# Four graph layers on one core: edges 2 gathers projected node rows of 768 bytes, and edges 0 takes 18 VectorE steps

## The chip, the cores and the metric

The kernel runs on one core of one Trainium2 chip. The metric is the time of one execution on the device in microseconds (us). The core has five engines that run side by side and meet at semaphores: TensorE (PE in the profile, its weight loads PEld), VectorE (DVE), ScalarE (ACT), GpSimd (POOL) and SyncE (SP), which here only issues DMAs. Sixteen DMA engines move the data. SBUF and PSUM are the two on-chip memories; TensorE writes only to PSUM.

## The reference

A graph of 12,500 nodes and 200,000 edges, sorted by their destination `dst`, goes through four layers, each followed by a sum with `x` and a layer norm. Every layer makes something per edge from a row of its source node and from edge attributes, sums it over each destination's edges (in three layers with a softmax over these edges), and does some work per node. The change is about the third layer, L2, and a little about the first, L0:

```python
# L0 (16 values per head, 4 heads)
scores = jnp.einsum('ehd,ehd->eh', q[edge_src], k[edge_dst]) / np.sqrt(D)
agg = segment_sum(softmax_over_dst(scores)[:, :, None] * v[edge_src], edge_dst)

# L2: h = x, eh = edge_attr_64, qrh = edge_attr_64_n2, qeh = edge_attr_64_n3, one head, d = 64
se = jnp.concatenate([h[src], eh], axis=-1)
msg = jax.nn.leaky_relu(se @ W_msg, 0.01)
q = jnp.concatenate([qrh, qeh], axis=-1) @ W_q / temp      # temp = 8
k = se @ W_k
att = jnp.sum(q * k, axis=-1)
alpha = softmax of att over the edges of each dst
agg = jax.ops.segment_sum(alpha[..., None] * msg, dst, num_segments=N)
hn = leaky_relu(agg @ W_out) + h    # then a layer norm; nodes without edges keep h
```

Everything is float32.

## The kernel before

**Stages.** The program is a row of blocks, one after the other: setup and search (indices, the q, k, v projections of L0), then for each layer an edge phase and a node phase: edges 0, nodes 0, edges 1, nodes 1, edges 2, nodes 2, edges 3, nodes 3. A block begins when all engines have ended the one before. Each partition holds 1,568 edges in a row and 98 nodes in a row (`edges_pp`, `nodes_pp`).

**An edge phase** (`class EdgePhase`) works in 56 chunks of `J` = 28 columns; a column is 128 edges, one per partition. For each column GpSimd issues one indirect DMA (L774) that gathers 128 rows of a table by source node: 1,568 gathers in a phase. The chunks alternate between two buffers `b`; a buffer is given back by the semaphore `rows_free[b]`. SP loads attributes and stores the running sums. VectorE and ScalarE make scores, a running maximum along the edges, exponentials, and a scan that sums over the edges of a destination; `lay_out` on ScalarE turns the sums around for the store to `sums`. After the last chunk, `Chained` repairs destinations whose edges lie in two partitions (L971 to L974), and only then does the node phase gather the last sum of every node: 98 gathers (L1671).

**Edges 2 before** (`edge_phase_2`, L1274): the gathers bring rows of `x` (64 floats, 256 bytes) from `p.x_tables[1]` into the left half of `se`; ScalarE copies the edge attribute into the right half (L1403). For each four columns (`QUAD`) TensorE turns `se` and the two query attributes (L1338, L1342), ScalarE moves them out of PSUM (L1386, L1387), TensorE multiplies with `w2_mk` (message and key side by side, L1356) and with `w2_qr`, `w2_qe` (L1358, L1359), ScalarE takes the results (L1394, L1396), and VectorE multiplies query and key (L1457), makes the leaky message from the PSUM tile and the copy `msg` (L1458) and reduces the score (L1461). Once per chunk follow the running softmax (L830 to L836), the weighting of `msg` (L1471) and five scans (L892). The last chunk is cut at column `ph.cut` = 20, so that its first part is summed and stored while the rest is made (`part_of_last`, L1478).

**Nodes 1 before** (`node_phase_1`, L2004) has two passes over 15 groups of nodes (13 of `G` = 7 columns, then 4 and 3). The first goes with the 98 gathers and collects the batch-norm sums. Then comes the point at which all engines need the moments (L2147 to L2174). The second pass: ScalarE applies scale and ReLU (`light`, L2102), TensorE turns back and centres (`turn_back`, L2075), VectorE adds to `x` (L2180), ScalarE squares (L1710), VectorE sums (L1715), ScalarE takes the root (L1720), VectorE inverts it (`turn_over`, L1733), GpSimd scales the rows (L2050), and SP stores them as the table for edges 2 (L1680). The order in which each engine takes these stages is set by `in_turn(groups, (lag, stage), ..., per=)`: stage `lag` steps behind, one group every `per` steps.

**Edges 0 before** (`edge_phase_0`, L1042): per chunk one scan per head for the running maximum (L830), one multiplication per head for the values (L1115), one scan per head for the sums (L892).

## Time and profile before

| what | value |
|---|---|
| median of 3 runs | 9007.13 us (9006.42 to 9010.77) |
| time of the profiled execution | 9015.53 us |
| its span, first to last instruction | 9013.6 us |
| edges 0, gathers by edge (335 to 2240) | 1905 us |
| edges 1 (2537 to 4499) | 1962 us |
| nodes 1 with the tail of edges 1 (4499 to 4714) | 215 us |
| edges 2 (4714 to 6677) | 1963 us |
| nodes 2 with the tail of edges 2 (6677 to 6888) | 211 us |
| edges 3 (6888 to 8845) | 1957 us |

Times within the trace are us from the start of the span. A row of an instruction gives its start, its duration, the engine, the line, what it writes from what, the shape, and in brackets how long its engine stood idle before it and for whom. Of GpSimd's instructions the gathers are the busy ones; "issue" is time in which it waited for nothing that the profile shows. A row such as `x8` holds eight instructions that follow each other. A float32 product on TensorE stands in the trace as two MATMUL instructions.

### The profile page before, as it was taken

How to read it: one execution, taken by the hardware profiler on the slowest of the kernel's cores; microseconds unless marked ns; L12 is line 12 of the kernel's file. 1: busy time of each engine (PE TensorE's matmuls, PEld its weight loads, DVE VectorE, ACT ScalarE, POOL GpSimd, SP SyncE). 2: the span in 40 equal slices, each digit the busy share in tenths (PEclk: the TensorE clock that was granted, in tenths of full speed). 3: DMA queues.
4: the chain of work that ended last, by engine and by line, in shares of the span. 5: the costliest groups of instructions: out<-in, count | busy, mean ns of one | idle time of the engine just before them, and what ended most of it. 6: DMA issues, size and time to landing. Idle time of an engine off the chain costs nothing. (4 is left out here: it accounts for less than half of the span.)

```text
span 9013.6 us, 55519 instructions
## 1 busy us (share of the span) xinstructions
PE 2221.6 (25%) x11915; PEld 1741.6 (19%) x11915; DVE 4945.2 (55%) x6681; ACT 3183.7 (35%) x3856; POOL 6621.2 (73%) x6997
## 2 busy tenths in 40 slices
PE   3000000000200000000046666666654222222224
PEld 1000000000200000000026666666643010101013
DVE  5356565656747777777744454544455333333335
ACT  0123222222513232232324555555544333333332
POOL 6777777777677777777757777777765777777776
PEclk6555555555555555555558888888877565656556
DMA  9233333333123333333323443434322333333332
GB/s 359 81 111 105 111 107 109 109 109 112 35 77 105 111 102 114 102 114 102 105 79 121 131 136 129 138 128 139 125 86 76 124 114 124 114 122 116 121 117 82
DMA packets 367105, 1037.47 MB, mean 115 GB/s; under 512 B 164320, under 2 KB 172410, under 8 KB 352272
## 3 DMA queue, kind: packets, MB, share of 16 engines
q1 hardware_dynamic: 136048, 670.35, 19.9%
q0 software_dynamic: 224608, 342.26, 15.6%
q10 hardware_dynamic: 6336, 23.79, 0.7%
q14 instruction: 96, 0.79, 0.0%
q8 instruction: 17, 0.28, 0.0%
HBM read 634.02 MB, written 401.90 MB: 115 GB/s over the span
## 5 line engine op out<-in xcount | busy, mean ns | idle before, releaser
L774 POOL DMA_INDIRECT g<-x_table,edge_ix x1512 | 1426.9, 944 | 460.8 <-issue 460.8
L774 POOL DMA_INDIRECT se<-x_table,edge_ix x1512 | 1426.8, 944 | 460.8 <-issue 460.8
L774 POOL DMA_INDIRECT hidden<-hidden_table,edge_ix x1512 | 1426.6, 943 | 460.8 <-issue 460.8
L774 POOL DMA_INDIRECT qv<-qv_table,edge_ix x1484 | 1400.3, 944 | 452.3 <-issue 452.3
L902 ACT ACTIVATE edge_sums<-edge_val 128x1904 f32<-128x1904 f32 (+3 forms) x220 | 1115.2, 5069 | 459.8 <-DVEq L1597 459.8
L892 DVE TENSOR_TENSOR_SCAN edge_val<-edge_bank,edge_val 128x464 f32<-128x464 f32 (+1 forms) x715 | 687.7, 1033 | 360.1 <-ACT edge_val L1559 353.6
L1551 PE MATMUL edge_e_ps<-w_nodes,edge_ea_t 128*128 128x512 f32 x784 | 477.9, 776 | 1464.6 <-DVEq L1591 1456.1
L845 ACT ACTIVATE edge_bank<-edge_weight_arg 128x112 f32<-128x112 f32 (+3 forms) x169 | 38.6, 228 | 2114.5 <-DVE edge_decay_arg L836 2114.5
L892 DVE TENSOR_TENSOR_SCAN edge_val<-edge_decay,edge_val 128x493 f32<-128x493 f32 (+1 forms) x672 | 714.2, 1132 | 13.4
L1590 DVE TENSOR_TENSOR hidden<-hidden,edge_e_ps 128x3584 f32<-128x3584 f32 x55 | 213.9, 3888 | 843.5 <-DMA hidden<-hidden_table,edge_ix 792.9
L1457 DVE TENSOR_TENSOR edge_product<-mk_ps,edge_q_now 128x256 f32<-128x256 f32 x392 | 166.5, 425 | 900.3 <-ACT edge_msg L1396 899.1
L1559 ACT ACTIVATE edge_val<-hidden 128x3584 f32<-128x3584 f32 x55 | 348.4, 6335 | 786.7 <-DVEq L1591 786.7
L1104 DVE TENSOR_TENSOR edge_product<-edge_k_ps,qv 128x896 f32<-128x896 f32 x112 | 185.7, 1658 | 642.4 <-DMA qv<-qv_table,edge_ix 635.4
L1551 PEld LDWEIGHTS edge_e_ps<-w_nodes,edge_ea_t 128*128 128x128 f32 x784 | 192.4, 254 | 1750.0 <-DVEq L1591 1501.6
L1029 PE MATMUL edge_k_ps<-ident,edge_fix_wide 128*128 128x128 f32 x8 | 2.1, 441 | 2092.7 <-DVEq L989 2092.7
L1356 PE MATMUL mk_ps<-w_mk,edge_se_t 128*128 128x128 f32 x3136 | 480.9, 302 | 141.9 <-ACT edge_q_t L1387 122.1
L1029 PE MATMUL edge_bond_ps<-ident,edge_fix_wide 128*128 128x128 f32 x4 | 1.2, 462 | 2041.7 <-DVEq L989 2041.7
L1671 POOL DMA_INDIRECT node_rows<-sums,end_index x392 | 374.9, 956 | 129.5 <-issue 118.2
L1356 PEld LDWEIGHTS mk_ps<-w_mk,edge_se_t 128*128 128x128 f32 x3136 | 429.8, 212 | 179.5 <-ACT edge_q_t L1387 140.8
L1338 PE MATMUL se_ps<-ident,se 128*128 128x128 f32 x1568 | 304.0, 327 | 535.9 <-ACT se L1403 354.1
L1029 PEld LDWEIGHTS edge_k_ps<-ident,edge_fix_wide 128*128 128x128 f32 x8 | 1.8, 328 | 2092.8 <-DVEq L989 2092.8
L1029 PEld LDWEIGHTS edge_bond_ps<-ident,edge_fix_wide 128*128 128x128 f32 x4 | 0.9, 323 | 2041.8 <-DVEq L989 2041.8
(418 smaller groups left out, 8264.4 us busy)
## 6 DMA issues: line engine op xcount, KB each, us to landing
sums<-edge_sums SPq DMA_DIRECT2D x56, 1848.0 KB, 7.1
sums<-edge_sums SPq DMA_DIRECT2D x55, 1792.0 KB, 6.3
sums<-edge_sums SPq DMA_DIRECT2D x56, 1008.0 KB, 4.3
sums<-edge_sums SPq DMA_DIRECT2D x55, 924.0 KB, 3.8
edge_k<-k_edges SPq DMA_DIRECT2D x56, 896.0 KB, 4.6
edge_bond<-in_edge_attr SPq DMA_DIRECT2D x56, 896.0 KB, 8.3
edge_eh<-in_edge_attr SPq DMA_DIRECT2D x56, 896.0 KB
edge_qr<-in_edge_attr_n SPq DMA_DIRECT2D x56, 896.0 KB
```

The source lines that it names most:

```text
L774: e.indirect_dma_start(self.gather_into(u, j), None, self.gather_from, bass.IndirectOffsetOnAxis(ap=now[:, j:j + 1], axis=0))\
L845: e.activation(self.weight[:, :, now], self.weight_arg[:, :, now], ACT.Exp).then_inc(self.weighed, 1)
L892: return e.tensor_tensor_scan(out=now, data0=keep[:, 0:n, :].rearrange("p f j -> p (f j)"), data1=now, initial=0.0, op0=ALU.mult, op1=ALU.add)
L902: e.activation(self.sums[b][:, :, 0:n], self.val[b][:, :, 1:].rearrange("p f j -> p j f"), ACT.Copy)\
L1104: e.tensor_tensor(product[:, 32 * half:32 * half + 32, :], k_ps[:, :, 1:], q[:, 32 * half:32 * half + 32, :], ALU.mult)
L1338: e.transpose(se_ps[u][:, j, :], se[b][:, QUAD * c + j, :], p.ident[:, :])
L1356: e.matmul(mk_ps[u][:, j, :], se_t[u][:, j, :], p.w2_mk[:, :], start=True, stop=True)
L1457: e.tensor_tensor(product[:, now, :], mk_ps[u][:, :, FD:], q_now[u][:, :, :], ALU.mult)
L1551: last = e.matmul(e_banks[:, q, :], ea_t[b][:, q, :], p.w3_e, start=True, stop=True)
L1559: e.activation(ph.val[b][:, :, 1:], g[b].rearrange("p j f -> p f j"), ACT.Relu).then_inc(taken, 1)
L1590: e.tensor_tensor(g[b][:, :, :], g[b][:, :, :], e_ps, ALU.add)
L1671: e.indirect_dma_start(self.rows[:, t, :], None, self.p.sums[self.layer], bass.IndirectOffsetOnAxis(ap=self.p.end_index[:, t:t + 1], axis=0))\
```

## The change

**Edges 2.** The score is rewritten: q · k = (attributes of the query) · (`W_q` `W_k`^T applied to `se`). Nodes 1 makes, for every node, a row of 192 floats, `x W_msg` (64) and `x W_k W_q^T / 8` (128, "points"), and stores it in `pair_table` (768 bytes a row). Edges 2 gathers these rows. TensorE makes only the part of the edge attribute, from attributes that are turned on the host (`eh_t`, one product of 384 columns for two columns of edges, `p.w2_e`), in six `pieces` of 4, 4, 6, 4, 4 and 6 columns over a ring of seven PSUM banks. VectorE adds the gathered points into the PSUM tile, adds the gathered message part into `msg` (SBUF), multiplies the points with the 128 query attributes (`q_in`, loaded as they are) and reduces. The leaky step is one instruction per chunk on `msg`, behind the running softmax. The transposes, ScalarE's copies and the query product are gone. `rows_free` and `attr_free` are now given by VectorE after the last piece. `cut` is 18.

**Nodes 1.** The weights are prepared at its start (loads, two transposes, two products, copies). The second pass gets, behind GpSimd's scaling, `turn_x` and `project` on TensorE and `move_x` and `take_x` on ScalarE; the store comes from `pair_out`. `in_turn` goes by `per=4`.

**Edges 0** (`merged=True`): one scan for the running maximum of all heads, one multiplication for all values, one scan for all sums; the penalty row is a copy per head in SBUF; the factor 0.25 moves from every chunk into the query weights in the setup, for which TensorE now waits (`s_quartered`). `part_summed` comes from the one scan.

```diff
@@ edge_phase_2 @@
-                e.tensor_tensor(product[:, now, :], mk_ps[u][:, :, FD:], q_now[u][:, :, :], ALU.mult)
-                e.scalar_tensor_tensor(msg[:, now, :], mk_ps[u][:, :, 0:FD], 0.01, msg[:, now, :],
-                                       ALU.mult, ALU.max).then_inc(scored, 1)
-                e.drain()
-                e.tensor_reduce(score[:, 0, now], product[:, now, :], AX.X, ALU.add)
+                e.wait_ge(made, at(i, 2 * per, per * b + k + 1))
+                e.tensor_tensor(points, two(g[b][:, cols, FD:]), points, ALU.add)
+                e.tensor_tensor(two(msg[:, cols, :]), two(g[b][:, cols, 0:FD]), values, ALU.add)
+                e.drain()
+                e.tensor_tensor(two(product[:, 0:slot, :]), two(q_in[b][:, cols, :]), points, ALU.mult)
+                e.drain().then_inc(used, 1)
+                e.tensor_reduce(ph.score[:, 0, cols], product[:, 0:slot, :], AX.X, ALU.add)
+                e.drain()
 
             def chunk(i, b):
...
+                for k in range(per):
+                    weigh(i, b, k)
+                e.sem_inc(ph.rows_free[b], 1)
+                e.sem_inc(ph.attr_free[b], 1)
                 ph.carry_values(e, i, b)
                 ph.running_softmax(e, i, b)
+                e.scalar_tensor_tensor(msg[:, :, :], msg[:, :, :], 0.01, msg[:, :, :], ALU.mult, ALU.max)
+                e.drain()
                 ph.wait_decay(e, i, b)
@@ node_phase_1, TensorE @@
+            def project(g):
+                e.wait_ge(x_moved, g + 1)
+                after(e, x_taken, g)
+                for k in range(firsts[g]):
+                    last = e.matmul(pair_banks[:, k, :], x_t[g % 2][:, k, :], p.w2_x, start=True, stop=True)
+                last.then_inc(x_done, 1)
-            in_turn(groups, (1, turn_back))
+            in_turn(groups, (1, turn_back), (8, turn_x), (10, project), per=4)
@@ node_phase_1, ScalarE @@
+            def move_x(g):
+                n = firsts[g]
+                e.wait_ge(x_turned, g + 1)
+                after(e, x_done, g - 1)
+                e.activation(x_t[g % 2][:, 0:n, :], x_ps[:, 0:n, :], ACT.Copy).then_inc(x_moved, 1)
             in_turn(groups,
                     (0, light),
                     (3, lambda g: norm.act_square(e, g, p.x[:, ph.now(g), :])),
-                    (5, lambda g: norm.act_root(e, g, p.eps[:, 0:1])))
+                    (5, lambda g: norm.act_root(e, g, p.eps[:, 0:1])),
+                    (9, move_x),
+                    (11, take_x), per=4)
@@ edge_phase_0 @@
-                    for n in range(4):
-                        last = ph.scan_rows(e, b, rows * n, rows, decay[:, n, :, :])
-                        if n == 1:
-                            last.then_inc(ph.part_summed, 1)
+                    sums = ph.val[b].rearrange("p f j -> p (f j)")
+                    e.tensor_tensor_scan(out=sums, data0=decay_flat, data1=sums, initial=0.0,
+                                         op0=ALU.mult, op1=ALU.add).then_inc(ph.part_summed, 1)
```

How the instructions stand now. ScalarE in the second pass of nodes 1, before (`node_held` is `light`, `node_rows` the square, `node_var` the root):

```order
L2102 ACTIVATE node_held<-node_held,node_bn 128x512 x3
L1710 ACTIVATE node_rows<-x_now 128x7x64
L2102 ACTIVATE node_held<-node_held,node_bn 128x512
L1710 ACTIVATE node_rows<-x_now 128x7x64
L2102 ACTIVATE node_held<-node_held,node_bn 128x512
L1720 ACTIVATE node_var<-node_var,eps 128x7
L1710 ACTIVATE node_rows<-x_now 128x7x64
```

The same place after; `node_x_t` is `move_x`, `node_pair_out` is `take_x`:

```order
L2088 ACTIVATE node_held<-node_held,node_bn 128x512
L2094 ACTIVATE node_x_t<-node_work 128x512
L1658 ACTIVATE node_var<-node_var,eps 128x7
L2102 ACTIVATE node_pair_out<-node_work 128x1152
L2105 ACTIVATE node_pair_out<-node_work 128x192
L1648 ACTIVATE node_rows<-x_now 128x7x64
L2088 ACTIVATE node_held<-node_held,node_bn 128x512
```

Three `light` instructions ran ahead before; now each stands behind the `take_x` of a group that is three behind it, with the square between them.

TensorE in the same pass, before and after; before there are only the 56 products of `turn_back`:

```order
L2081 MATMUL node_fold_ps<-node_moments,node_fold 128x2
L2082 MATMUL node_fold_ps<-node_moments,node_fold 128x1
L2075 MATMUL node_back_ps<-node_centred,node_held 128x128 x56
```

```order
L2043 MATMUL node_work<-ident,x_now 128x128 x3
L2046 MATMUL node_work<-ident,x_now 64x128
L2035 MATMUL node_back_ps<-node_centred,node_held 128x128 x4
L2053 MATMUL node_work<-w_nodes,node_x_t 128x384 x4
L2043 MATMUL node_work<-ident,x_now 128x128 x3
L2046 MATMUL node_work<-ident,x_now 64x128
L2035 MATMUL node_back_ps<-node_centred,node_held 128x128 x4
L2053 MATMUL node_work<-w_nodes,node_x_t 128x384 x4
```

`turn_x` of a group, `turn_back` of the group two ahead and `project` of the group now follow each other.

VectorE in edges 2, before, the steps of one `QUAD` (`edge_product` is query times key, `edge_score` the reduced score):

```order
L1457 TENSOR_TENSOR edge_product<-mk_ps,edge_q_now 128x256
L1458 SCALAR_TENSOR_TENSOR edge_msg<-mk_ps,edge_msg 128x256
L1461 TENSOR_REDUCE edge_score<-edge_product 128x4
```

After, from the last piece of a chunk to the weighting of the messages:

```order
L1389 TENSOR_TENSOR edge_pair_ps<-pair,edge_pair_ps 128x3x2x128
L1390 TENSOR_TENSOR edge_msg<-pair,edge_pair_ps 128x384
L1392 TENSOR_TENSOR edge_product<-edge_q_in,edge_pair_ps 128x768
L1394 TENSOR_REDUCE edge_bank<-edge_product 128x6
...
L855 TENSOR_TENSOR edge_decay_arg<-edge_bank,edge_peak 128x28
L1404 SCALAR_TENSOR_TENSOR edge_msg<-edge_msg 128x1792
...
L1407 TENSOR_TENSOR edge_val<-edge_msg,edge_bank 128x64x28
```

The leaky step was made seven times a chunk from a PSUM tile; it now stands once, behind the running softmax, and reads `msg` alone.

## Rows read from the trace of the kernel before

**Rows 1.** The page's first part: busy time, share, instructions of each engine.
```profile
PE 2221.6 (25%) x11915; PEld 1741.6 (19%) x11915; DVE 4945.2 (55%) x6681; ACT 3183.7 (35%) x3856; POOL 6621.2 (73%) x6997
```
**Rows 2.** Busy time by stage: stretch, length, engines (instructions), clock, DMA share, GB/s.
```profile
4499.00:4714.00 215.00, 89.31 (x284) 52.17 (x284) 88.26 (x185) 53.20 (x101) 107.93 (x116) 0.60 0.22 64
4714.00:6677.00 1963.00, 1298.52 (x9368) 1224.81 (x9368) 961.34 (x1947) 999.30 (x1893) 1485.02 (x1568) 0.86 0.41 132
6888.00:8845.00 1957.00, 477.92 (x784) 192.43 (x784) 724.40 (x612) 714.95 (x111) 1479.41 (x1568) 0.60 0.37 118
```
**Rows 3.** Groups of gathers; the last is that of nodes 1, rows of 528 bytes.
```profile
L774 POOL DMA_INDIRECT se<-x_table,edge_ix x1512 | 1426.8, 944 | 460.8 <-issue 460.8
L774 POOL DMA_INDIRECT hidden<-hidden_table,edge_ix x1512 | 1426.6, 943 | 460.8 <-issue 460.8
...
L1671 POOL DMA_INDIRECT node_rows<-sums,end_index x98 | 92.6, 945 | 31.9 <-issue 29.6 <-POOLq L1169 2.4
```
**Rows 4.** Timeline of nodes 1, a group in the second pass, then its end.
```profile
4695.08 0.80 ACT L2102 ACTIVATE node_held<-node_held,node_bn 128x512 f32<-128x512 f32 x1
4696.20 0.58 ACT L1710 ACTIVATE node_rows<-x_now 128x448 f32<-128x448 f32 x1
4696.27 1.13 PE L2075 MATMUL node_back_ps<-node_centred,node_held 128*128 128x128 f32 x8 [0.47 <-DVE x_now L2180]
4696.68 0.80 ACT L2102 ACTIVATE node_held<-node_held,node_bn 128x512 f32<-128x512 f32 x1
...
4705.74 2.87 POOL L2050 TENSOR_TENSOR x_now<-x_now,node_var 128x448 f32<-128x448 f32 x4 [0.40 <-DVEq L1734]
...
4713.81 0.99 POOL L774 DMA_INDIRECT se<-x_table,first_src  x1 [5.21 <-POOLq L2498]
```
**Rows 5.** The second pass as two stretches: all of it, and its steady middle.
```profile
4680.60:4713.80 33.20, 16.90 (x112) 14.81 (x112) 19.62 (x48) 21.73 (x45) 13.17 (x15) 0.81 0.26 97
4689.00:4699.00 10.00, 7.23 (x53) 6.06 (x51) 8.48 (x20) 9.33 (x20) 5.99 (x7) 1.00 0.37 137
```
**Rows 6.** Prices: products of 512 columns in setup at either clock, ScalarE copies.
```profile
21.57 5.44 PE L597 MATMUL proj_ps<-w_nodes,x_t 128*128 128x512 f32 x8
...
27.28 3.60 PE L597 MATMUL proj_ps<-w_nodes,x_t 128*128 128x512 f32 x8
...
L1386 ACT ACTIVATE edge_se_t<-se_ps 128x512 f32<-128x512 f32 x392 | 234.1, 597 | 319.2 <-PE q_ps L1342 302.5 <-issue 8.8 <-DVEq L1449 7.9
...
L2068 PE MATMUL node_h_ps<-node_tile_t,node_w_pair 128*128 128x384 f32 x26 | 19.1, 837 | 0.0
```
**Rows 7.** Timeline: VectorE with both inputs in SBUF, and gathers.
```profile
4720.74 2.03 DVE L1445 TENSOR_TENSOR edge_product<-bc_L_gnn_beta,live 128x1792 f32<-128x1792 f32 x1
4721.35 2.25 POOL L774 DMA_INDIRECT se<-x_table,first_src  x1 [0.30 <-issue]
4722.85 2.03 DVE L1448 TENSOR_TENSOR aux_now<-aux_now,edge_product 128x1792 f32<-128x1792 f32 x1
4723.91 1.78 POOL L774 DMA_INDIRECT se<-x_table,first_src  x1 [0.30 <-issue]
...
6743.91 0.62 DVE L2306 SCALAR_TENSOR_TENSOR node_other<-node_other 128x448 f32<-128x448 f32 x1
6744.09 1.26 POOL L1671 DMA_INDIRECT node_rows<-sums,end_index  x1 [0.30 <-issue]
```
**Rows 8.** VectorE groups in edges 2, and in edges 0 (last).
```profile
L892 DVE TENSOR_TENSOR_SCAN edge_val<-edge_bank,edge_val 128x377 f32<-128x377 f32 x275 | 235.3, 922 | 6.4
L1471 DVE TENSOR_TENSOR edge_val<-edge_msg,edge_bank 128x1792 f32<-128x1792 f32 x55 | 179.0, 3255 | 42.4 <-ACT edge_bank L848 42.4
L1461 DVE TENSOR_REDUCE edge_score<-edge_product 128x4 f32<-128x256 f32 x392 | 164.7, 420 | 36.3
...
L1115 DVE TENSOR_TENSOR edge_val<-qv,edge_bank 128x448 f32<-128x448 f32 x220 | 185.7, 906 | 18.3 <-ACT edge_bank L845 18.3
```
**Rows 9.** Timeline of the end of edges 2.
```profile
6675.65 0.95 POOL L774 DMA_INDIRECT se<-x_table,edge_ix  x1 [0.30 <-issue]
...
6694.48 0.33 SPq L742 DMA_DIRECT2D sums<-edge_sums  x1
...
6705.37 0.97 POOL L1671 DMA_INDIRECT node_rows<-sums,end_index  x1 [2.29 <-POOLq L1280]
```

More of the change, by code:

```diff
@@ L1374, in _ @@
+                    for k, cols in enumerate(pieces):
+                        e.wait_ge(used, at(i, 2 * per, per * b + k + 1))
+                        for n, bank in enumerate(range(slots[k % ring].start, slots[k % ring].stop)):
+                            last = e.matmul(banks[:, bank, 0:2 * wide], eh_t[b][:, cols.start // 2 + n, :],
+                                            p.w2_e[:, :], start=True, stop=True)
+                        last.then_inc(made, 1)
             chained.tensor(e)
@@ L1480, in part_of_last @@
                 i, now = ph.rounds - 1, ph.columns(more)
-                for c in range(now.start // QUAD, now.stop // QUAD):
-                    weigh(i, 1, c)
-                e.drain()
-                e.tensor_scalar(ph.score[:, :, now], score[:, :, now], 0.125, None, ALU.mult)
+                for k in range(per):
+                    if now.start <= pieces[k].start < now.stop:
+                        weigh(i, 1, k)
                 e.memset(cut_decay(more)[:, :, :, 0], 0.0)
@@ L2038, in _ @@
         def _(e):
-            for g in range(groups):
-                ph.store(e, g, p.x_tables[1])
-            e.wait_ge(ph.out, 16 * groups)
+            e.dma_start(w_k[:, :], p.ins["L2_gnn_W_k"]).then_inc(w_in, 16)
+            e.dma_start(w_q[:, :], p.ins["L2_gnn_W_q"]).then_inc(w_in, 16)
+            e.wait_ge(w_zeroed, 1)
+            for n in range(2):
+                for k, to in enumerate((p.w2_x, p.w2_e)):
+                    e.dma_start(to[n * FD:(n + 1) * FD, n * wide:n * wide + FD],
+                                p.ins["L2_gnn_W_msg"][k * FD:(k + 1) * FD, :]).then_inc(w_in, 16)
+            table = p.pair_table.rearrange("(p t) f -> p t f", p=P)
+            for g in range(groups):
+                e.wait_ge(x_taken, g + 1)
+                e.dma_start(table[:, ph.now(g), :], pair_out[g % outs][:, 0:ph.sizes[g], :])\
+                    .then_inc(stored[g % outs], 16)
+            for u in range(outs):
+                e.wait_ge(stored[u], 16 * len(range(u, groups, outs)))
         @block.gpsimd
```

321 lines of the change are left out of this document (158 added, 163 removed).

## Prediction

> **What bounds the kernel.** I began with the page's busy line [rows 1]: GpSimd is busy 73% of the span, no other engine more than 55%. That is an average, so next came busy time by stage [rows 2]. In edges 2, 1,963 us long, GpSimd is busy for 1,485 us with 1,568 gathers, TensorE for 1,299, ScalarE for 999, VectorE for 961. The groups of instructions [rows 3] give the rest of GpSimd's time: a gather is busy for 944 ns, and in front of each lie 460.8/1,512 = 0.305 us of "issue", in which it waits for nobody. 0.944 + 0.305 = 1.249 us, times 1,568 is 1,958 us: the whole stage. So edges 2 is a bare stream of gathers, and edges 3 is the same stream (943 ns, 1,957 us) with TensorE at 478 us instead of 1,299. What the change takes from TensorE and ScalarE in edges 2 lies behind this stream and is worth nothing there. Three things count: what lies between streams, what delays GpSimd inside one, and what would outgrow the 35.0 us that 28 gathers take.
>
> Between the streams I read the timeline of nodes 1 [rows 4]. From the point at which all engines have the moments (4680.60) to the first gather of edges 2 (4713.81) lie 33.2 us [rows 5] in which GpSimd has only 15 short scalings. No gather can start before the last row of the table is stored, so each microsecond added here is a microsecond of the kernel.
>
> **Edges 2, the stream.** Rows grow from 256 to 768 bytes. The trace has 256 bytes (944 ns), 512 (943) and 528 (945) [rows 3]: no slope, so 0 is taken. The mean DMA share is 0.41 with rows of 256 bytes and 0.37 with 512 and fewer attributes [rows 2]; tripled rows bring it to about 0.55 by my estimate, with room left. A loss, if transfers did back up, is a rival below.
>
> VectorE per chunk: with both inputs in SBUF 448 elements take 0.62 us and 1,792 take 2.03 [rows 7], so 1.05 ns an element and 0.15 fixed. A piece of 4 columns is three instructions over 512 elements and one over 256: 3 x 0.69 + 0.42 = 2.5, 2.65 with its drains; a piece of 6 by the same 3.6. Four and two of them are 17.8 us. Then the small instructions of the softmax with their waits for ScalarE, about 1.9 (an estimate), the leaky step 2.0, the weighting 3.26 and five scans 235.3/55 = 4.3 [rows 8]: 29.3 us of 35.0. Hidden, with 5.7 us to spare; TensorE's 14 products of 384 columns, 28 instructions at 0.73 us even at half clock [rows 6], are 20 us, hidden too.
>
> **The leaky step delays a gather.** In before it read PSUM and `msg`; now it reads `msg` twice, 1,792 columns, 2.03 us. At the start of edges 2 the timeline [rows 7] shows what such an instruction does: VectorE runs from 4720.74 to 4722.77 with both inputs in SBUF, and the gather begun at 4721.35 takes 2.25 us, not 0.94; it ends 0.83 us behind VectorE. The second pair (4722.85 + 2.03; 4723.91 + 1.78) ends 0.81 behind, and in nodes 2 an instruction of 0.62 us from 6743.91 makes the gather of 6744.09 take 1.26, again 0.82 behind. So a gather needs something 0.13 us after its start, and if VectorE is in such an instruction then, it waits for its end. Within the chunks of before only instructions with an input in PSUM run, and the gathers keep their 944 ns [rows 3]. The new step comes once in each of 55 whole chunks. If its phase against the gathers is random, a gather starts 0 to 1.249 us into it; the stretch is what is left of 2.03, on average 2.03 - 0.62 = 1.4 us: **+77 us**. The phase is in fact nearly fixed within a chunk, since VectorE starts its last piece on the last gather's landing; my sum for the step's start, about 7.6 us behind that, falls right beside a gather's need, and I can't tell which side. The ends are 0.78 us a chunk (+43) and 2.0 (+111).
>
> **Nodes 1, second pass.** Before, a group costs 1.6 us (`light` 4695.08 to 4696.68 [rows 4]), TensorE being in its 8 instructions for 1.13 of it. The middle shows 7.23 us of TensorE in 10 at clock 1.00 [rows 5]. After, ScalarE's order puts `light` of a group behind `take_x` of one three behind, `take_x` waits for `project`, and TensorE's order puts `project` behind the `turn_back` that needs that `light`. That closes a ring with no overlap:
> take_x, 1,152 and 192 columns, by 0.597 for 512 [rows 6]: 1.5; square 0.5; light 0.75; turn_back 1.13; project, 8 instructions of 384 columns, by 3.60/8 x 384/512 = 0.34 each: 2.7. That is 6.6, with five hand-overs of 0.1 **7.1 us a group**. At half clock turn_back is about 2.0 and project 8 x 0.66 = 5.3 (between 0.51 = 5.44/8 x 0.75 and 0.73 [rows 6]): 10.6 us.
> TensorE is in the ring's work (turn_back, project, and turn_x beside take_x) for some 5 of 7.1 us, the share that stands beside full clock in [rows 5], so I take the warm price. The pass: two groups of filling 8.1, one cycle in which group 0 goes down its whole chain (norm, scaling 2.87, transpose, move) 9.2, twelve cycles 85.2, less 1.3 for the two short groups, the last project and take 5.2, and from there to the first gather 5.2 as before's last wait [rows 4]. Together 111.6 us instead of 33.2: **+78.5**. Below: if the ring overlapped fully, TensorE's 5.1 us a group would bound it, some 88 us, +55. Above: at half clock twelve cycles cost 3.5 more each, +120.
>
> **Small terms.** The weights' preparation at the start of nodes 1 lies beside 98 gathers (98 x 1.25 = 122 us [rows 3]): 0. In setup TensorE waits for two more VectorE scalings, some 2.5 us; VectorE's and GpSimd's later idle time takes it up: 0, at most 1. Edges 0: `lag` now reads SBUF twice for about 0.3 us a chunk; by the rule above it would rarely meet the need of a gather, 0 taken, at most 15. Its nine fewer instructions a chunk are hidden but in the last; between 0 and 9 x 0.15 I take -0.6. The tail of edges 2: before, the store goes out at 6694.48, 17.9 us after the last gather's end [rows 9]. After, on the same clock: the cut part is done by 6678.8 (my sum, from the landing of its last column), two pieces 6.25, softmax 1.5, leaky 0.8, weighting 1.2, scans 1.8, turning around 1.2: 6691.6, **-2.9**.
>
> **Sum.** Profiled execution 9015.5 + 78.5 + 77 - 2.9 - 0.6 = 9167.5, +152. That execution is 8.4 us above the median of 9007.1, so the median becomes 9159 us.
>
> **Rivals.**
> 1. The clock stays at its half level in the second pass: the ring has waits that before's middle has not. The whole pass stands at 0.81 [rows 5], nodes 1 as a whole at 0.60 [rows 2]. +120 instead of +78.5: about 9200.
> 2. VectorE becomes the bound in edges 2, or rows of 768 bytes back up. For it: 5.7 us of margin rest on estimates, and PSUM accesses may cost more than SBUF's. Each microsecond a chunk over 35.0 costs 56 us, so one that is over by 1 gives 9215, and up from there. Against: the sum of 29.3 would have to be off by a fifth.
> 3. No stretch, because the leaky step falls where no gather needs anything or the rule is something else: 9159 - 77 = 9082.
> 4. Not slower. ScalarE's 999 us and TensorE's 1,299 in edges 2 slow each gather, and without them its 1.249 us shrinks. To cancel 152 us it must lose 152/1,568 = 97 ns; with 1.15 us the time is about 9004. Against: edges 3 has 715 and 478 us of the same work and the same 943 ns [rows 2, 3].
> 5. The change doesn't do what it says, for instance the ring isn't closed because the order of the two engines leaves slack: +55 instead of +78.5, 9136; this is inside the forecast's own range.
>
> **How the numbers follow.** Forecast (with 5) 0.72, clock 0.09, VectorE or transfers 0.08, no stretch 0.07, not slower 0.04. The forecast's own bounds are the stretch at 43 or 111 and the pass at +55 or +78.5: 9102 to 9193. The range takes in the missing stretch below and the low clock with a long stretch above, 9080 to 9225. A run of this kernel can tell 0.2%, 18 us, from no change. Only rival 4 comes there: faster 0.03, same 0.02; slower 0.95.
>
> **What would show it.** The stretch: in edges 2 one gather a chunk of 1.7 to 2.9 us, ending about 0.8 behind the leaky step, all others at 944 ns; GpSimd busy about 1,560 us and the stage about 2,040. The pass: first gather of edges 2 about 110 us behind the moments, ScalarE's `light` every 7.1 us, its wait ended by TensorE's `project`. I am wrong if VectorE and not "issue" ends GpSimd's idle time in edges 2, if gathers without a VectorE instruction beside them differ from 944 ns, or if the pass shows half clock.

## The result and the profile after

| what | before | after |
|---|---|---|
| median of 4 runs, us | 9008.95 | 9134.59 |
| lowest and highest | 9006.42, 9013.25 | 9130.21, 9136.48 |
| ratio, 95% interval | | 1.0137 (1.0124 to 1.0150) |
| span of the profiled execution | 9013.6 | 9132.2 |

The changed kernel is 1.4% slower, 125.6 us in the medians against 152 forecast. The spans of the two profiled executions differ by 118.6 us. By the first and last gathers of the stages, that difference lies here:

| stretch | before, us | after, us | difference |
|---|---|---|---|
| start to the end of the last gather of nodes 1 | 4666.9 | 4668.9 | +2.0 |
| from there to the first gather of edges 2 (contains the second pass) | 46.9 | 118.6 | +71.8 |
| first to last gather of edges 2 | 1962.8 | 2017.3 | +54.5 |
| tail of edges 2, to the first gather of nodes 2 | 28.8 | 25.1 | -3.7 |
| nodes 2, to the first gather of edges 3 | 182.6 | 178.9 | -3.7 |
| edges 3 and nodes 3 | 2125.6 | 2123.3 | -2.3 |

The last two rows are code that the change doesn't touch. Their 6.0 us are about the 6.6 us by which before's profiled execution lies above the median of its runs. The row of nodes 2 wanders by that much in any case: in the four variants of the next section, where its code is the same, it is 178.1 to 181.8 us. The page's busy line, to be held against [rows 1]:

```profile
PE 1872.5 (21%) x4249; PEld 957.9 (10%) x4249; DVE 5454.6 (60%) x6299; ACT 2476.6 (27%) x2302; POOL 6676.1 (73%) x6997
```

Three stages in the windows view, against [rows 2] (stretch, length, busy time and instructions of TensorE, its weight loads, VectorE, ScalarE, GpSimd, then clock, DMA share, GB/s):

```profile
4501.00:4787.50 286.50, 141.59 (x458) 84.17 (x458) 92.03 (x193) 78.31 (x146) 107.78 (x116) 0.67 0.21 71
4787.50:6805.00 2017.50, 916.40 (x1568) 419.43 (x1568) 1510.68 (x2130) 269.31 (x305) 1539.94 (x1568) 0.67 0.53 179
7008.80:8966.00 1957.20, 476.39 (x784) 192.34 (x784) 725.41 (x612) 715.20 (x111) 1479.52 (x1568) 0.60 0.36 118
```

In edges 2 TensorE lost 382 us of work and ScalarE 730, VectorE gained 549, and the stage is as long as GpSimd's stream makes it: 2,017.5 instead of 1,963, with GpSimd 55 us busier. Its groups of gathers (against [rows 3]: 944 ns, 460.8 us of issue):

```profile
L783 POOL DMA_INDIRECT pair<-pair_table,edge_ix x1512 | 1480.5, 979 | 460.6 <-issue 460.6
L783 POOL DMA_INDIRECT g<-x_table,edge_ix x1512 | 1427.9, 944 | 460.8 <-issue 460.8
```

The issue time is what it was; the mean of a gather is 979 ns. In the view of the gathers' one line, the minimum, median and maximum of the same gathers show that this is no slope with the row size, but a few long ones:

```profile
L783 POOL DMA_INDIRECT pair<-pair_table,edge_ix x1512: 942/946/2046, 4864.1 to 6804.0; - x189
```

One chunk's timeline shows where the long one stands (start, duration):

```profile
5265.47 0.95 POOL L783 DMA_INDIRECT pair<-pair_table,edge_ix  x1 [0.30 <-issue]
5265.71 0.19 DVE L855 TENSOR_TENSOR edge_decay_arg<-edge_bank,edge_peak 128x28 f32<-128x28 f32 x1
5265.81 2.01 DVE L1404 SCALAR_TENSOR_TENSOR edge_msg<-edge_msg 128x1792 f32<-128x1792 f32 x1
...
5266.72 1.92 POOL L783 DMA_INDIRECT pair<-pair_table,edge_ix  x1 [0.30 <-issue]
```

The leaky step runs to 5267.82; the gather of 5266.72 needs something at 5266.85 and ends 0.98 us late, at 5268.64, which is 0.82 behind the step's end, as in [rows 7]. All 55 steps do this, with stretches of 0.84 to 1.10 us, 51.2 us in all. The other 3 us of the stage are the median of a gather, 946 instead of 944 ns, times 1,568.

The second pass of nodes 1, ScalarE's timeline of one group (against [rows 4]):

```profile
4743.35 1.13 ACT L2102 ACTIVATE node_pair_out<-node_work 128x1152 f32<-128x1152 f32 x1 [3.15 <-PE node_work L2053]
4744.38 0.33 ACT L2105 ACTIVATE node_pair_out<-node_work 128x192 f32<-128x192 f32 x1
4744.59 0.58 ACT L1648 ACTIVATE node_rows<-x_now 128x448 f32<-128x448 f32 x1
4745.05 0.81 ACT L2088 ACTIVATE node_held<-node_held,node_bn 128x512 f32<-128x512 f32 x1
...
4749.69 1.13 ACT L2102 ACTIVATE node_pair_out<-node_work 128x1152 f32<-128x1152 f32 x1 [3.15 <-PE node_work L2053]
```

And TensorE's, of the same group and of one 13 us later:

```profile
4745.92 1.16 PE L2035 MATMUL node_back_ps<-node_centred,node_held 128*128 128x128 f32 x8 [2.17 <-ACT node_held L2088]
4746.91 2.75 PE L2053 MATMUL node_work<-w_nodes,node_x_t 128*128 128x384 f32 x8
...
4758.61 1.87 PE L2035 MATMUL node_back_ps<-node_centred,node_held 128*128 128x128 f32 x8 [2.17 <-ACT node_held L2088]
4760.28 3.74 PE L2053 MATMUL node_work<-w_nodes,node_x_t 128*128 128x384 f32 x8
```

The ring is there: ScalarE waits 3.15 us for `project`, TensorE 2.17 us for `light`, and `take_x` comes every 6.34 us (4743.35, 4749.69). The last two rows are a group in which `turn_back` and `project` take 1.87 and 3.74 us instead of 1.16 and 2.75; every third or fourth group is such a one. The windows view gives the granted clock of the two groups, 1.00 and 0.72 (third number from the end):

```profile
4745.90:4752.20 6.30, 4.18 (x20) 2.80 (x20) 1.45 (x3) 3.15 (x7) 0.94 (x1) 1.00 0.26 108
4758.60:4764.80 6.20, 5.84 (x20) 3.95 (x20) 0.82 (x2) 1.38 (x3) 0.94 (x1) 0.72 0.21 84
```

### The profile page after: what moved, and what is told of

Its sections match the earlier page's. It is cut to its first block and busy times, and to the rows that moved or that the text cites. A ratio compares the mean times of both kernels' runs of the same rounds, so it can differ in the third digit from the quotient of the medians.

```text
span 9132.2 us, 36460 instructions
## 1 busy us (share of the span) xinstructions
PE 1872.5 (21%) x4249; PEld 957.9 (10%) x4249; DVE 5454.6 (60%) x6299; ACT 2476.6 (27%) x2302; POOL 6676.1 (73%) x6997
## 5 line engine op out<-in xcount | busy, mean ns | idle before, releaser
L783 POOL DMA_INDIRECT pair<-pair_table,edge_ix x1512 | 1480.5, 979 | 460.6 <-issue 460.6
L783 POOL DMA_INDIRECT g<-x_table,edge_ix x1512 | 1427.9, 944 | 460.8 <-issue 460.8
L783 POOL DMA_INDIRECT hidden<-hidden_table,edge_ix x1512 | 1426.7, 944 | 460.8 <-issue 460.8
L1340 PE MATMUL edge_pair_ps<-w_e,edge_eh_t 128*128 128x384 f32 x1568 | 916.4, 749 | 1101.4 <-DVEq L1393 1086.3
L1340 PEld LDWEIGHTS edge_pair_ps<-w_e,edge_eh_t 128*128 128x128 f32 x1568 | 419.4, 287 | 1597.8 <-DVEq L1393 1329.5
L1389 DVE TENSOR_TENSOR edge_pair_ps<-pair,edge_pair_ps 128x512 f32<-128x512 f32 x336 | 263.8, 785 | 401.1 <-DMA pair<-pair_table,edge_ix 315.0
L911 DVE TENSOR_TENSOR_SCAN edge_val<-edge_decay,edge_val 128x493 f32<-128x493 f32 x448 | 467.4, 1117 | 6.7
L920 ACT ACTIVATE edge_sums<-edge_peak 128x112 f32<-128x112 f32 (+2 forms) x165 | 50.2, 304 | 1269.9 <-DVEq L1257 669.8
L1228 DVE TENSOR_TENSOR g<-g,edge_bond_ps 128x1792 f32<-128x1792 f32 x56 | 113.2, 2021 | 430.4 <-DMA g<-x_table,edge_ix 394.7
L1246 DVE TENSOR_TENSOR edge_val<-g,edge_bank 128x1792 f32<-128x1792 f32 x112 | 351.6, 3179 | 16.1 <-ACT edge_bank L864 16.1
```

Source lines behind the costliest of these rows:

```text
L783: e.indirect_dma_start(self.gather_into(u, j), None, self.gather_from, bass.IndirectOffsetOnAxis(ap=now[:, j:j + 1], axis=0))\
L911: return e.tensor_tensor_scan(out=now, data0=keep[:, 0:n, :].rearrange("p f j -> p (f j)"), data1=now, initial=0.0, op0=ALU.mult, op1=ALU.add)
L1228: e.tensor_tensor(g[b][:, :, :], g[b][:, :, :], bond_ps[:, :, :], ALU.add)
L1246: e.tensor_tensor(ph.values(b)[:, n, :, :], rows_now, bcast(ph.weight[:, n, :], 1, FD), ALU.mult)
L1340: last = e.matmul(banks[:, bank, 0:2 * wide], eh_t[b][:, cols.start // 2 + n, :], p.w2_e[:, :], start=True, stop=True)
L1389: e.tensor_tensor(points, two(g[b][:, cols, FD:]), points, ALU.add)
```

## Experiments on the two terms

Four variants of the changed kernel ran on one chip, where the kernel before took 9,009.2 us; beside the changed kernel itself, 9,134.59 us, it had taken 9,008.95. Theory A: a gather needs something 0.13 us after its start, and then waits for the end of a VectorE instruction that is running with both inputs in SBUF. The rivals: the time that VectorE spends in such instructions counts, wherever it stands (B), or any long VectorE instruction does it (C).

**The leaky step in two parts.**

```diff
-                e.scalar_tensor_tensor(msg[:, :, :], msg[:, :, :], 0.01, msg[:, :, :], ALU.mult, ALU.max)
-                e.drain()
+                for m in (msg[:, 0:13, :], msg[:, 13:J, :]):
+                    e.scalar_tensor_tensor(m, m, 0.01, m, ALU.mult, ALU.max)
+                    e.drain()
```

> The changed kernel, with the leaky step of edges 2 in two instructions, of 13 and 15 of the 28 columns, at the same place. In the trace of the changed kernel each of the 55 steps stretches one gather by 0.84 to 1.11 us, 51 us in all; the step of 5265.81 + 2.01 meets the gather of 5266.72. Theory A (a gather needs something 0.13 us after its start, and waits for the end of the VectorE instruction with two SBUF inputs that is running just then): the first part would run from 5265.81 to 5266.83, the gather needs at 5266.85, the second part would run from about 5266.9 to 5268.05, the next gather needs at 5268.10. Both parts miss, the stretch falls from 0.93 to 0 to 0.15 us a chunk, and the time falls by 43 to 51 us, to about 9087. Theory B (what counts is how long VectorE reads two SBUF inputs beside a gather, wherever the gather stands): the same 2.1 us a chunk, the same 51 us, the time stays within 5 us of 9135.

Measured 9084.13 us, 50.5 less than the changed kernel. One chunk's timeline:

```profile
5327.53 0.95 POOL L783 DMA_INDIRECT pair<-pair_table,edge_ix  x1 [0.30 <-issue]
...
5327.91 2.25 DVE L1405 SCALAR_TENSOR_TENSOR edge_msg<-edge_msg 128x832 f32<-128x832 f32 x2
...
5328.78 0.95 POOL L783 DMA_INDIRECT pair<-pair_table,edge_ix  x1 [0.30 <-issue]
5330.04 0.94 POOL L783 DMA_INDIRECT pair<-pair_table,edge_ix  x1 [0.30 <-issue]
```

The page's group of the gathers:

```profile
L783 POOL DMA_INDIRECT pair<-pair_table,edge_ix x1512 | 1429.9, 946 | 460.5 <-issue 460.5
```

VectorE spends 2.25 us here, more than before the split, and no gather of the chunk is stretched by more than 0.01 us: the first part (1.01 us) ends at 5328.92, the gather needs at 5328.91, and the second part ends at 5330.16, where the next gather needs at 5330.17. The mean over all chunks is 946 ns, as the median. B falls.

**The leaky step 0.45 us sooner**, directly behind the scan of the running maximum instead of three short instructions later.

> The changed kernel, with the leaky step moved ahead by two short instructions, to directly behind the scan of the running maximum: it starts 0.45 us sooner, at 5265.36 instead of 5265.81 on the clock of that chunk, and ends 5267.37. Theory A: the gather that starts at 5265.47 needs something at 5265.60, now inside the step, and waits until 5267.37: a stretch of 1.77 us a chunk instead of 0.93, so 46 us more than the changed kernel, about 9180 (with a jitter of the phase of 0.15 us, 9170 to 9190). Theory B (duration alone counts) and the theory that gathers are slowed by rows of 768 bytes: no difference, 9135.

Measured 9180.71 us, 46.1 more than the changed kernel. The chunk:

```profile
5349.20 2.02 DVE L1405 SCALAR_TENSOR_TENSOR edge_msg<-edge_msg 128x1792 f32<-128x1792 f32 x1
5349.30 2.75 POOL L783 DMA_INDIRECT pair<-pair_table,edge_ix  x1 [0.30 <-issue]
```

The same instruction, moved by less than half a microsecond, now holds the gather from 5349.43 to 5351.22: 1.79 us, and over 55 chunks 95.9 us.

**One input in PSUM.** The step becomes a maximum of `msg` with a row of a PSUM bank, of the same length (2.01 us) at the same place. The variant leaves the leaky step out, so it doesn't compute the reference, and TensorE gets the bank of the last piece back only behind this instruction (`used`); the part of the edit that holds it back is left out here.

```diff
...
-                e.scalar_tensor_tensor(msg[:, :, :], msg[:, :, :], 0.01, msg[:, :, :], ALU.mult, ALU.max)
-                e.drain()
+                e.tensor_tensor(msg[:, :, :], msg[:, :, :], bcast(banks[:, slots[-1].start, 0:FD], 1, J), ALU.max)
+                e.drain().then_inc(used, 1)
```

> The changed kernel, with the leaky step of edges 2 replaced, at the same place, by a maximum of the same 1,792 elements with 64 values of a PSUM bank, repeated over the columns: same length, one input in SBUF, one in PSUM. It leaves the leaky step out. Theory A (two SBUF inputs are what a gather waits for): all gathers of the chunks back at 0.94 to 0.95 us, 51 us less, about 9084. Theory C (any long VectorE instruction at this place, or VectorE's load as a whole, holds the gather up): the same stretch, 9135.

Measured 9086.79 us, 47.8 less. The four runs lie between 9082.44 and 9103.45, and the profiled one is the longest; in it gathers have a median of 947 ns in stages that no edit touches too, 949 in edges 2. The chunk shows a gather that starts inside the instruction and keeps its length; so do those of all 55 chunks:

```profile
5336.91 2.01 DVE L1407 TENSOR_TENSOR edge_msg<-edge_msg,edge_pair_ps 128x1792 f32<-128x1792 f32 x1
...
5337.90 0.94 POOL L783 DMA_INDIRECT pair<-pair_table,edge_ix  x1 [0.30 <-issue]
```

C falls as well: at the same length and the same place, the second SBUF input makes the difference.

**Where theory A is wrong.** It says that a gather is held if its need, 0.13 us after its start, falls inside the instruction. In the trace of `leaky_split` there are 20 gathers whose need does fall inside the second part, but which start 0.02 to 0.13 us before it. One of them, and the second part beside it:

```profile
5363.78 0.95 POOL L783 DMA_INDIRECT pair<-pair_table,edge_ix  x1 [0.30 <-issue]
5363.87 1.16 DVE L1405 SCALAR_TENSOR_TENSOR edge_msg<-edge_msg 128x960 f32<-128x960 f32 x1
```

By theory A this gather waits from 5363.91 to 5365.03, and the 20 together are 22 us longer; none of them takes more than 0.95 us. Nine others start inside the first part with their need still ahead of its end, and are 0.29 us longer in all, where theory A gives 0.26. So the rule that the traces bear out has one more condition: a gather is held only if it starts while the instruction is running, and then until the instruction's end, from 0.13 us after the gather's start. The gain of the split rests on both, the needs at the ends of the parts and the gathers that were already under way when the second part began.

**The second pass in another order.** Only the lags change (turn_back 6, turn_x 16, project 21; light 1, square 10, root 12, move_x 16, take_x 23; add_x 7, sum 10, turn_over 12), so that `light` runs a group further ahead and `turn_x` and `move_x` of the next group stand before `project` and `take_x` of this one.

> The changed kernel, with another order in the second pass of nodes 1 and nothing else: light, turn_back and the norm run one group further ahead, turn_x of the next group stands before project of this one, and move_x before take_x. The trace of the changed kernel shows 6.35 us a group at full clock (every fourth or fifth about 8 us), in which ScalarE waits 3.15 us for project and TensorE 2.17 us for light. Theory A (the ring take_x, square, light, turn_back, project is what makes the pass long): without it TensorE is the bound, project 2.75, turn_back 1.16, turn_x 0.66 = 4.6 us a group, 5.1 with the slower groups: 11 groups x 1.85 = 20 us less, and up to 5 more at the ends; about 9110. Rival (the clock: with less waiting nothing else changes, but TensorE's work itself is the bound): nothing, 9135.

Measured 9106.94 us, 27.7 less; the first gather of edges 2 comes 88.2 us after the last of nodes 1 instead of 118.6. The windows row of the pass:

```profile
4682.60:4756.70 74.10, 59.02 (x274) 39.96 (x273) 20.72 (x48) 45.25 (x87) 13.29 (x15) 0.96 0.32 130
```

Two rounds of TensorE in its timeline:

```profile
4716.20 2.82 PE L2053 MATMUL node_work<-w_nodes,node_x_t 128*128 128x384 f32 x8 [0.21 <-ACT node_pair_out L2105]
4718.85 1.05 PE L2035 MATMUL node_back_ps<-node_centred,node_held 128*128 128x128 f32 x8
4719.75 0.49 PE L2043 MATMUL node_work<-ident,x_now 128*128 128x128 f32 x3
...
4720.55 2.82 PE L2053 MATMUL node_work<-w_nodes,node_x_t 128*128 128x384 f32 x8 [0.21 <-ACT node_pair_out L2105]
```

A group takes 4.35 us, TensorE waits 0.21 of them. The ring was worth 2.0 us a group; what is left is TensorE's own work. The slower groups are gone too, all twelve rounds between `take_x` of full groups are 4.35 us: the granted clock of the stretch is 0.96, where the pass of the changed kernel has this row:

```profile
4682.60:4787.60 105.00, 67.53 (x277) 45.32 (x276) 21.08 (x48) 45.90 (x89) 13.32 (x16) 0.89 0.23 92
```

## Runs on other chips

The other eight runs fell on four other chips, in four groups, and on each of them the kernel before takes 11,422 to 11,443 us. A time of these runs is compared only with that of before on the same chip. Gathers don't bound edges 2 of before on these chips, as shown below, so the times say little for or against the expectations that were made for a chip with 9,009 us.

> The kernel before, with one instruction added in each of the 55 whole chunks of edges 2, where the changed kernel has its leaky step: a maximum of msg with itself, 1,792 elements, two SBUF inputs, about 2.0 us. It changes no value. VectorE has some 17 us to spare in a chunk. Theory A (a gather waits from 0.13 us after its start to the end of such an instruction): from the trace of before it would start at 5325.30 in one chunk and end 5327.31, and the gather of 5326.06 needs at 5326.19: 1.12 us; in the chunk of 6023.45 the gather of 6023.97 would wait 1.36. So 62 to 75 us more than before, about 9078. Theory D (the step costs only in the changed kernel, whose rows of 768 bytes or whose VectorE load make gathers touchy): at most 5 us, 9009 to 9014.

> The kernel before, with the instructions of two SBUF inputs at the starts of edges 1 and edges 2 given one input in PSUM: the two scans of 1,568 elements that read same (copied to PSUM first), and beta times live and its addition to aux, in thirteen steps of eight nodes through PSUM. In before's trace these stretch gathers by 2.94 + 2.07 = 5.0 us in edges 1 and by six times 0.84 to 1.31 = 5.5 us in edges 2. Theory A: both go, 10 us less, about 8999. Rival (the copies and the additional steps hold up the first chunk instead): no change or up to 5 us more.

> The kernel before with the part of edges 0 and the setup alone: one scan for the running maximum, one multiplication, one scan for the sums, the factor 0.25 in the query weights. My prediction had 0 for the setup, 0 (at most +15) for the new addition of two SBUF inputs, and -0.6 for the tail. The trace of the changed kernel has the first gather of edges 0 0.6 us later, the stream itself 0.1 us shorter and the nodes' first gather 0.35 us later relative to it: +0.8 in all. Either way the time stays within 2 us of before; the trace tells which.

> The changed kernel with the leaky step in two parts, the other order in the second pass of nodes 1, and the starts of edges 1 and 2 without instructions of two SBUF inputs. If the three are independent: 9134.6 - 50.5 (as measured for the split) - 27.7 (as measured for the order) - 10 = 9046. If the stretches were one budget that something else then fills, or the phase of the chunks shifts so that the parts of the leaky step meet a gather again, up to 50 us more. In no case below before: the projection's TensorE time in nodes 1, some 40 us, stays.

> The kernel before with one maximum of msg with itself added in each of the 55 whole chunks of edges 2, at the place of the changed kernel's leaky step: 1,792 elements, two SBUF inputs, about 2.0 us; no value changes. It is run again because the chip of the first run has longer times throughout (11,425 us for the kernel before), with GpSimd waiting for TensorE in edges 2; this one is to tell on a chip with 9,009 for before. Theory A (a gather waits from 0.13 us after its start to the end of such an instruction): 1.12 and 1.36 us in the two chunks read in before's trace, so 62 to 75 us more than before, about 9078. Theory D (the step costs only in the changed kernel): at most 5 us, 9009 to 9014.

> The changed kernel with the leaky step in two parts, the other order in the second pass of nodes 1, and the starts of edges 1 and 2 without instructions of two SBUF inputs; again for the same reason. If the three are independent: 9134.6 - 50.5 - 27.7 - 10 = 9046. If the phase of the chunks shifts so that the parts of the leaky step meet a gather again, up to 50 us more. On a chip with 11,425 for before it should again be near 10,400.

> The changed kernel as it is, next to the kernel before. On the chip of the last two groups of runs before takes 11,425 to 11,443 us, and there edges 2 is not a stream: GpSimd pauses some 27 us in each chunk, for TensorE to give a buffer back. If what pauses it is the long way from a landed row through transposes, ScalarE and TensorE, the changed kernel, in which VectorE gives the buffer back behind six short pieces, gains there what the three variants together gained: 10,400 to 10,600 us, some 8% less than before. If that gain came from the three edits of the variant, the changed kernel is near before. On a chip with 9,009 for before it is 9,130 to 9,137 again.

> The kernel before with edges 0 and the setup as in the changed kernel, and with the starts of edges 1 and 2 free of instructions of two SBUF inputs: what the runs so far leave as candidates for a version below both kernels. On a chip with 9,009 us for before: the quiet starts take away 5.0 + 5.5 us of stretched gathers, the part of edges 0 adds 0.8: 9 to 10 us less, 8,999 to 9,001. On a chip with 11,425 for before: the part of edges 0 alone measured 20 us less there, the quiet starts alone nothing (0.9999): 11,405, ratio 0.998. If neither holds, no difference.

| kernel | us | before on the chip | ratio (95% interval) |
|---|---|---|---|
| changed kernel (changed_again) | 10419.8 | 11421.9 | 0.9126 (0.9111 to 0.9141) |
| changed, three edits (split_open_quiet) | 10402.3 | 11425.5 | 0.9102 (0.9090 to 0.9114) |
| the same (all_three_again) | 10429.1 | 11442.9 | 0.9113 (0.9098 to 0.9128) |
| before plus an instruction (before_two_sbuf) | 11275.1 | 11425.5 | 0.9866 (0.9851 to 0.9881) |
| the same (two_sbuf_again) | 11329.1 | 11442.9 | 0.9897 (0.9881 to 0.9914) |
| quiet starts (before_quiet) | 11424.9 | 11425.5 | 0.9999 (0.9990 to 1.0008) |
| edges 0 part alone (edges0_only) | 11405.3 | 11425.5 | 0.9983 (0.9974 to 0.9992) |
| edges 0 part and quiet starts (quiet_edges0) | 11415.8 | 11443.2 | 0.9977 (0.9968 to 0.9986) |

Of the expectations, that of `changed_again` came (10,400 to 10,600), and so did the ratio of 0.998 for `quiet_edges0`; `all_three_again` was to be near 10,400 and is 10,429. The added instruction was to cost 62 to 75 us and before got 150 and 114 us faster; the edges 0 part was to stay within 2 us and is 20 us faster; the quiet starts were to give 10 us and gave 0.6. In the trace of `before_quiet` the six long gathers at the start of edges 2 are indeed gone, which `edges0_only` on the same chip has (5.5 us in all), and the time doesn't follow.

**The changed kernel is 8.7% faster there.** The profile tells where, not why. These are the windows rows of edges 2, first gather to the end of the last one. No trace of before itself was kept there, so the first row is that of `before_quiet`, which makes edges 2 in the same way; it and the changed kernel ran on two chips, with 11,425.5 and 11,421.9 us for before:

```profile
5262.40:8640.90 3378.50, 1383.97 (x9112) 1325.04 (x9112) 941.11 (x1919) 963.34 (x1840) 1480.10 (x1568) 0.69 0.23 76
```

The changed kernel:

```profile
5319.40:7653.00 2333.60, 890.74 (x1541) 386.42 (x1542) 1478.03 (x2079) 264.35 (x297) 1551.83 (x1568) 0.64 0.47 154
```

Edges 2 takes 3,378 us in the one and 2,334 in the other, with the same 1,568 gathers: 1,045 us less. The way from the last gather of nodes 1 to it takes 75 us more (87.4 and 162.2), and the stages around it give 34 back; the gain is 1,002 in the medians. Edges 2 of before is no stream of gathers here. GpSimd's wait in it (in total, times, longest):

```profile
POOL se L774 <- PEq L1348: 1408.0, 53, 27.8
```

And in the changed kernel:

```profile
POOL pair L783 <- DVEq L1395: 308.7, 26, 15.2
```

In before it waits once a chunk for TensorE to give the rows back, up to 27.8 us; in the changed kernel it waits for VectorE, 26 times. During the wait of 27.8 us ScalarE's timeline in before reads so:

```profile
5561.84 0.60 ACT L1388 ACTIVATE edge_se_t<-se_ps 128x512 f32<-128x512 f32 x1 [8.89 <-remote]
5562.33 0.59 ACT L1389 ACTIVATE edge_q_t<-q_ps 128x512 f32<-128x512 f32 x1
5580.79 0.38 ACT L1396 ACTIVATE edge_q_now<-qo_ps 128x256 f32<-128x256 f32 x1 [17.86 <-DMA picked<-in_dst_table,found_row_u]
```

And TensorE's:

```profile
5554.67 0.39 PE L1361 MATMUL qo_ps<-w_qe,edge_q_t 128*128 128x128 f32 x2
...
5555.55 0.38 PE L1344 MATMUL q_ps<-ident,edge_qe 128*128 128x128 f32 x2
5581.55 0.77 PE L1358 MATMUL mk_ps<-w_mk,edge_se_t 128*128 128x128 f32 x2 [25.62 <-issue]
```

TensorE had made the products that ScalarE takes at 5580.79 by 5555.1, and the transposes that it takes at 5561.84 by 5555.9. ScalarE stands still twice, 8.9 and 17.9 us, with nothing to wait for that the profile shows (the names given there belong to the setup), and VectorE and TensorE stand still behind it. ScalarE has 107 waits above 5 us in edges 2 of this trace, two in a chunk; on the first chip before has two in the whole stage. The changed kernel has 297 instructions of ScalarE in edges 2 instead of 1,840. Its products and pieces need no copy by ScalarE, so that the way to the buffer's return passes through it only at the exponentials of the chunk before, for which VectorE waits. That this is why it gains is argued, not shown. The edits to edges 2 were not tried one by one on these chips. Other stages that the change leaves alone are longer there as well: edges 3 of `before_quiet` takes 2,168 us instead of 1,957, with gathers of 1.07 us in the mean, and its edges 0 2,140 instead of 1,905, with gathers of 0.948 and more idle time between them. What makes ScalarE stop on these chips, and why an added VectorE instruction of 2 us makes before 1.0 to 1.3% faster there, stays open; nothing here separates it.

**Theory A on before.** The two runs with the added instruction can't show its price in time, since gathers don't bind edges 2 on these chips. Their traces show its effect on single gathers:

```profile
5783.10 2.02 DVE L1470 TENSOR_TENSOR edge_msg<-edge_msg 128x1792 f32<-128x1792 f32 x1
5783.49 2.44 POOL L774 DMA_INDIRECT se<-x_table,edge_ix  x1 [0.30 <-issue]
```

The need at 5783.62, the end at 5785.12: 1.50 us, and 2.44 - 0.94 = 1.50 is what the gather is longer. 54 gathers are stretched, by 78.0 us in all, with rows of 256 bytes and an instruction with two SBUF inputs as the only thing added; the 55th instruction comes after the last gather. So D, by which this would be a matter of the changed kernel alone, falls for the stretch; that the time follows on the first chips stays argued for before, and shown for the changed kernel. The condition on the start shows here too, with an instruction of full length:

```profile
6428.59 0.95 POOL L774 DMA_INDIRECT se<-x_table,edge_ix  x1 [0.30 <-issue]
6428.67 2.01 DVE L1470 TENSOR_TENSOR edge_msg<-edge_msg 128x1792 f32<-128x1792 f32 x1
...
6429.85 1.65 POOL L774 DMA_INDIRECT se<-x_table,edge_ix  x1 [0.31 <-issue]
```

The gather of 6428.59, begun 0.08 us before the instruction, keeps its 0.95 us, though its need would be at 6428.72; the next one, begun inside, is held by 0.70. Four gathers of this trace start like the first, and none is longer.

**The parts.** The three edits of the changed kernel change next to nothing here: 0.9102 and 0.9113 beside 0.9126, with intervals that overlap. Whether they add up on a chip of the first kind, to the 9,046 us that I worked out, wasn't measured. Edges 0's part is 0.17% faster; the first gather of nodes 0 comes 20.6 us sooner than in the variant with quiet starts on the same chip (2515.4 against 2536.0). Together with the quiet starts it is 0.23% faster than before. It, the edges 0 part alone and the two runs with the added instruction are faster than before on these chips and keep its way of making edges 2; all are far behind the changed kernel there. On the first kind none of them was tried.

## The prediction, point by point

- **What bounds it** held on the first chips: edges 2 is GpSimd's stream in both kernels, and 1,112 us less work on TensorE and ScalarE gave nothing. Gathers of 768 bytes that no instruction disturbs have a median of 946 ns, against 944 with 256 bytes.
- **The leaky step** was the right mechanism, and its size was the term that was most off: +77 taken, +51.2 in the changed kernel's trace, 50.5 by the run that splits it. What failed is "if its phase is random". I had seen that the phase is nearly fixed and had put the step's start about 7.6 us behind "that", by its words the last gather's landing; it lies beside a need only if it is counted from that gather's start (6 x 1.249 + 0.13 = 7.62). Counted so, the step starts at 7.84 (5257.97 to 5265.81). The gather begun at 7.50 is past its need by then; the one begun at 8.75 starts inside the step, and 0.98 us remain. The end that I had named for this side, 0.78 a chunk, was nearer than the mean. `leaky_sooner` is the other side, 1.74 a chunk. The mean was too high besides, since a gather that starts before the step isn't held: what is left at the need of one that starts inside it is on average 2.01 - 0.62 - 0.13 = 1.26 us, 69 us for 55 chunks by my estimate from the rows above.
- **The rule on two SBUF inputs.** The Trainium skill, page "SBUF — State Buffer", section "Who interferes with whom", lets a VectorE instruction with two SBUF inputs contend with a GpSimd instruction that reads SBUF. The one-PSUM variant agrees: 47.8 us go with the second SBUF input. That `tensor_tensor` can't starve the issue of a GpSimd DMA, as I had read the page, doesn't hold for these gathers: a `tensor_tensor` lengthens 54 of them above. Whether it is the reading of the indices that waits or something else in the gather, no row shows.
- **The ring of the second pass** was right in kind and in place: ScalarE waits for `project`, TensorE for `light`. 7.1 us a group was too much for full clock (6.34; the hand-overs of 0.1 and the overlap of `take_x`'s second instruction), and close to the mean of 6.96 that the slower groups make (4690.84 to 4767.37 in eleven groups, by GpSimd's scalings). From the moments to the first gather: 106.9 us, 111.6 forecast. That the sum came so near is partly luck: the ring's period was too long for full clock, and the slower groups, which it didn't have, made up for it. The clock: I had full or half; it is full with a slower group every third or fourth (0.72 in the one shown).
- **Small terms.** Tail of edges 2 -3.7 (taken -2.9). Setup and edges 0: the nodes' first gather 0.8 later (taken -0.6). Start of nodes 1 hidden, as said. VectorE 1,510.7/56 = 27.0 us a chunk, 29.3 forecast; DMA share 0.53, forecast 0.55.
- **The base.** The sum started from an execution that lay 6.6 us above the median of all runs of before (9015.5 and 9008.9); I took 8.4 off for it, from the median of the three runs that I had, and that was right in kind: the untouched stages gave 6.0 back.
- **The rivals** on the first chips: the clock at half level, VectorE as a bound, no stretch and a shorter period didn't come; the open ring, named as a fifth, was not what the change has, but what it could have had: `open_ring` gives its +55 - 78.5 = -23.5 as -27.7.
- **What no step had**: that the time before, and the bound, are other ones on other chips, and the sign with them. The argument "edges 2 is a bare stream" is one about the profile that I read.

## What to carry to other kernels

Where a stream of GpSimd gathers is the bound, look for each VectorE instruction with two SBUF inputs beside it: it costs not its duration but what is left of it when a gather that starts inside it needs something, so one of 2.0 us cost 0 in two parts, 0.93 in place and 1.74 half a microsecond sooner. In a hand-written order of stages, write down who waits for whom over one round; a closed ring over two engines cost 2 us a group here and went away by changed lags alone. And a change can cost 1.4% on one chip and gain 8.7% on another, as this one did: time it, and before beside it, on more than one chip before it is dropped or kept.

## What I had not expected

- The contention is sharp: 55 of 55 leaky steps stretch exactly one gather, each to within 0.01 us of the step's end less the gather's start less 0.13. A gather that started 0.02 us before such an instruction wasn't held. VectorE's phase against the gathers is fixed to 0.3 us over 1,900 us, since its last piece of each of the 55 chunks stands waiting, for at least 1.8 us, until the last gather has landed.
- The four chips with 11,422 to 11,443 us for before, against 9,009: edges 2 is 3,378 us instead of 1,963, and edges 1 2,168 (2836.7 to 5004.7) instead of 1,962, in the trace of `before_quiet`.
- The pass with less waiting had more clock: 0.96 instead of 0.89 in the second pass of nodes 1, with the same products.
